# Causal attention on one Trainium2 core: whole-array sums of values and ones, half-wise signals, and a moved output multiply

## The reference

```python
def _L1_attn_ref(x, g1, Wq, Wkv, Wout, g2):
    xn = layernorm(x, g1)
    q = xn @ Wq.T                      # 16 heads of 64
    kv = xn @ Wkv.T
    k, v = (kv[..., :DIM_HEAD], kv[..., DIM_HEAD:])
    ...
    q, k = (l2norm(q), l2norm(k))
    q, k = (q * srt, k * srt)          # srt = 4
    sim = jnp.einsum('bhid,bjd->bhij', q, k)
    causal_mask = jnp.triu(jnp.ones((n, n), dtype=bool), 1)
    sim = jnp.where(causal_mask, max_neg, sim)
    attn = jax.nn.softmax(sim.astype(jnp.float32), axis=-1).astype(sim.dtype)
    out = jnp.einsum('bhij,bjd->bhid', attn, v)
    out = out.transpose(0, 2, 1, 3).reshape(b, n, HEADS * DIM_HEAD)
    return layernorm(out @ Wout.T, g2)
x = _layernorm(x + _L1_attn_ref(x, ...), axis=-1)
```

## Time and profile before

| | us |
|---|---|
| median of 3 runs | 3532.06 |
| lowest and highest of them | 3529.45, 3533.05 |
| the profiled execution | 3527.5 |
| its span, first to last instruction | 3525.8 |
| ACT in the span | 2002.8 busy (57%) |
| DVE | 1776.7 busy (50%) |
| PE | 3118.4 busy (88%) |

### The profile page before, as it was taken

One profiled execution on the slowest core, in us unless ns is written; L12 is line 12 of the kernel. 1 busy time (PEld: TensorE's weight loads), 2 busy tenths in 40 slices (PEclk: granted clock), 3 DMA queues, 4 the chain that ended last, 5 costly groups with the idle time before them and its releaser, 6 DMA issues. The chain is left out here.

```text
span 3525.8 us, 44249 instructions
## 1 busy us (share of the span) xinstructions
PE 3118.4 (88%) x12438; PEld 1661.3 (47%) x12438; DVE 1776.7 (50%) x2639; ACT 2002.8 (57%) x3736; POOL 1152.1 (33%) x954
## 2 busy tenths in 40 slices
PE   5777777789999999966669999999998879999999
PEld 2333332257777777732224444444444634444443
DVE  5888888845555555569953333333333321111110
ACT  4666666446666666635657777777775523333333
POOL 4766776612222222236633333333332000000000
PEclk8999999989999999988889999999999989999999
DMA  3444444300000000001100000000000310000000
GB/s 108 136 137 131 136 138 134 106 16 22 21 16 21 18 20 21 14 27 51 45 36 10 14 17 13 13 13 18 13 13 27 125 42 18 18 21 24 18 18 15
DMA packets 104264, 159.17 MB, mean 45 GB/s; under 512 B 11904, under 2 KB 44560, under 8 KB 104208
## 3 DMA queue, kind: packets, MB, share of 16 engines
q1 hardware_dynamic: 97872, 144.89, 12.5%
q10 hardware_dynamic: 6336, 13.60, 1.4%
HBM read 85.77 MB, written 4.72 MB: 26 GB/s over the span
## 5 line engine op out<-in xcount | busy, mean ns | idle before, releaser
L1364 POOL TENSOR_TENSOR d_pr<-d_pr,d_keep 128x512 f32<-128x512 f32 x256 | 320.5, 1274 | 565.6 <-ACT d_pr L1522 565.6
L779 POOL TENSOR_TENSOR b_pn<-b_e,b_inv 128x616 f32<-128x616 f32 x128 | 161.5, 1261 | 602.9 <-DVE b_inv L960 602.9
L257 POOL TENSOR_TENSOR a_bx<-a_bcopy,a_drive_u 128x512 f32<-128x512 f32 x256 | 320.2, 1268 | 18.8 <-DVE a_state L532 18.0
L532 DVE TENSOR_TENSOR_SCAN a_state<-a_decay,a_bx 128x512 f32<-128x512 f32 x256 | 310.9, 1214 | 1.3 <-POOL a_bx L257 1.3
L277 PE MATMUL a_py<-a_prod,consts 128*128 128x512 f32 x512 | 296.7, 664 | 3.8 <-DVE a_t L512 3.1
L449 ACT ACTIVATE a_decay<-a_delta,neg_a 128x508 f32<-128x508 f32 x256 | 174.4, 683 | 145.3 <-DVE a_state L532 143.6
L1917 PE MATMUL f_ph<-f_hb,wb 128*128 128x512 f32 x512 | 232.8, 599 | 6.4 <-ACT f_hb L1952 6.4
L1917 PE MATMUL f_ph<-f_ha,wb 128*128 128x512 f32 x512 | 229.0, 596 | 2.3 <-DVE f_ha L1981 2.3
L289 PE MATMUL a_pc<-a_bc,sel 96*128 96x512 bf16 x256 | 109.9, 429 | 126.2 <-DVE a_prod L538 124.5
L935 DVE TENSOR_REDUCE b_peak<-b_pscore 128x8 f32<-128x616 f32 x128 | 102.3, 799 | 214.2 <-PE b_pscore L816 214.2
L885 ACT ACTIVATE b_yy<-b_py,y_bias 128x154 f32<-128x154 f32 x512 | 169.4, 382 | 66.2 <-PE b_py L825 66.0
(11 more groups left out here) (282 smaller groups left out, 6563.8 us busy)
## 6 DMA issues: line engine op xcount, KB each, us to landing
a_bcopy<-rows SPq DMA_DIRECT2D x256, 256.0 KB, 3.3
wb<-in_wb ACTq DMA_DIRECT2D x14, 480.0 KB, 3.7
a_xf<-in_x SPq DMA_DIRECT2D x16, 256.0 KB, 3.7
a_xt<-in_x ACTq DMA_DIRECT2D x16, 256.0 KB, 2.9
x<-a_xo SPq DMA_DIRECT2D x16, 256.0 KB, 3.6
b_xf<-x SPq DMA_DIRECT2D x32, 128.0 KB, 2.0
b_xt<-x SPq DMA_DIRECT2D x32, 128.0 KB, 2.0
x<-b_xo SPq DMA_DIRECT2D x32, 128.0 KB, 2.0
```

Of the source, the lines that this page charges most:

```text
L257: gp.tensor_tensor(bx[:, k % 4, :], bcopy[:, k % 4, :], drive_u[:, p, :], ALU.mult).then_inc(*bxt.step("bx"))
L532: V.tensor_tensor_scan(state[:, j % 2, :], decay[j % 2][:], bx[:, j % 4, :], 0.0, ALU.mult, ALU.add).then_inc(*vs.step("scan"))
L779: gp.tensor_tensor(heads(pn[:, j % 2, :]), heads(e[:, j % 2, :]), over(inv[:, j % 2, :], CTX), ALU.mult).then_inc(*pnt.step("n"))
L1364: gp.tensor_tensor(half, half, keep[:].unsqueeze(1).to_broadcast([128, QP, SEQ]), ALU.mult).then_inc(*gmt.step(f"m{odd}"))
```

## The change

It edits `causal_phase` alone.

1. **The sums.** d_vv holds three blocks of 64 columns per sequence, ones, values, ones; POOL fills all of it with ones at the start of the phase, and DVE copies the values into the middle block. `weighted` now has one matmul with 128 stationary columns for the even heads (blocks values, ones) into the first bank of a two-bank d_pattn, and one for the odd heads (blocks ones, values) into the second. Sums and weighted values lie on opposite halves of the partitions in each bank. d_pden and d_ones are gone.
2. **Signals.** Each of the two matmuls has its own signal, a0 and a1. The sums' Ln on ACT is two instructions on 64 partitions each, the first behind a0, the second behind a1; each reads one half of the partitions and writes the other half. The multiply on DVE is two instructions on 64 partitions.
3. **Squares.** Apart from the key's, the squares move to the tick of the projection (QUERY, odd k) and stand between the Ln halves and the Exp of the sums.
4. **Output.** The multiply into d_xo goes from the end of tick 7 to its start on DVE.

```diff
-        vv = sb("vv", [128, 2, NB, DH])
-        ones = sb("ones", [128, DH])
+        vv = sb("vv", [128, 2, NB, 3, DH])
...
-        pattn = ps("pattn")
-        pden = ps("pden")
+        pattn = ps("pattn", 1024)
...
-        pea = tr("pea", "a")
+        pea = tr("pea", "a0 a1")
...
-                gp.memset(ones[:], 1.0).then_inc(*made.step("ones"))
+                gp.memset(vv[:], 1.0).then_inc(*made.step("ones"))
...
-                    for bank, w in ((pattn, vv[:, p, b, :]), (pden, ones[:])):
-                        for odd in range(2):
-                            op = mm(bank[64 * odd:64 * odd + 64, :], w, pr[:, j % 2, odd, :], start=True, stop=True,
-                                    skip_group_check=True)
-                    op.then_inc(*pea.step("a"))
+                    for odd in range(2):
+                        w = vv[:, p, b, 1 - odd:3 - odd, :].rearrange("p i d -> p (i d)")
+                        mm(pattn[:, 512 * odd:512 * (odd + 1)], w, pr[:, j % 2, odd, :], start=True, stop=True
+                           ).then_inc(*pea.step(f"a{odd}"))
...
-                        if u := piece(LENGTH, g, p, k, front, main):
-                            squares(*u)
+                        if k == 3:
+                            if u := piece(LENGTH, g, p, k, front, main):
+                                squares(*u)
...
-                            A(den[:], pden[:], ACT.Ln).then_inc(*sdt.step("ln"))
+                            for odd in range(2):
+                                act.wait_ge(*pea.at(f"a{odd}", r))
+                                op = A(den[64 * odd:64 * odd + 64, :],
+                                       pattn[64 - 64 * odd:128 - 64 * odd, 512 * odd:512 * (odd + 1)], ACT.Ln)
+                            op.then_inc(*sdt.step("ln"))
+                        if k % 2:
+                            if u := piece(QUERY, g, p, k, front, main):
+                                squares(*u)
+                        if done:
                             act.wait_ge(*sdt.at("ln", r))
                             A(den[:], den[:], ACT.Exp, scale=-1.0).then_inc(*sdt.step("inv"))
...
+                        if tail and k == 7:
+                            dve.wait_ge(*so.at("rstd2", g - 1))
+                            if begun(g - 2):
+                                dve.wait_ge(store, 16 * g - 16)
+                            V.tensor_tensor(xo[:, q, :], pm[:, 0:N], t3[:], ALU.mult).then_inc(*vo.step("out"))
...
-                            V.tensor_copy(vv[:, q, :, :], pn[:, 0:NB * DH].rearrange("p (b d) -> p b d", b=NB)
+                            V.tensor_copy(vv[:, q, :, 1, :], pn[:, 0:NB * DH].rearrange("p (b d) -> p b d", b=NB)
...
-                            V.tensor_tensor(attn[:, pu, QP * hh:QP * (hh + 1), SEQ * b:SEQ * (b + 1)],
-                                            pattn[:].rearrange("p (i t) -> p i t", i=QP),
-                                            den[:].rearrange("p (i t) -> p i t", i=QP), ALU.mult
-                                            ).then_inc(*vat.step("n"))
+                            for odd in range(2):
+                                half = slice(64 * odd, 64 * odd + 64)
+                                op = V.tensor_tensor(
+                                    attn[half, pu, QP * hh:QP * (hh + 1), SEQ * b:SEQ * (b + 1)],
+                                    pattn[half, 512 * odd:512 * (odd + 1)].rearrange("p (i t) -> p i t", i=QP),
+                                    den[half, :].rearrange("p (i t) -> p i t", i=QP), ALU.mult)
+                            op.then_inc(*vat.step("n"))
...
-                        if tail and k == 7:
-                            dve.wait_ge(*so.at("rstd2", g - 1))
-                            if begun(g - 2):
-                                dve.wait_ge(store, 16 * g - 16)
-                            V.tensor_tensor(xo[:, q, :], pm[:, 0:N], t3[:], ALU.mult).then_inc(*vo.step("out"))
```

More of the change, by code:

```diff
@@ L1519, in step @@
                             if begun(r - 2):
-                                act.wait_ge(*pea.at("a", r - 2))
+                                act.wait_ge(*pea.at("a1", r - 2))
                             for odd in range(2):
@@ L1523, in step @@
                                   ).then_inc(*ext.step(f"e{odd}"))
-                        if u := summed(g, p, k, main, tail):
-                            _, _, j, r = u
-                            act.wait_ge(*pea.at("a", r))
+                        done = summed(g, p, k, main, tail)
+                        if done:
+                            _, _, j, r = done
                             if begun(r - 1):
                                 act.wait_ge(*vat.at("n", r - 1))
-                            A(den[:], pden[:], ACT.Ln).then_inc(*sdt.step("ln"))
+                            for odd in range(2):
[6 more added lines that the diff above has]
+                                squares(*u)
+                        if done:
                             act.wait_ge(*sdt.at("ln", r))
@@ L1575, in step @@
                             if begun(g - 1):
-                                dve.wait_ge(*pea.at("a", UNITS * g - 1))
-                            V.tensor_copy(vv[:, q, :, :], pn[:, 0:NB * DH].rearrange("p (b d) -> p b d", b=NB)
+                                dve.wait_ge(*pea.at("a1", UNITS * g - 1))
+                            V.tensor_copy(vv[:, q, :, 1, :], pn[:, 0:NB * DH].rearrange("p (b d) -> p b d", b=NB)
                                           ).then_inc(*vf.step("v"))
```

## The result

The changed kernel is slower, by little but clear of the scatter: 3550.85 us (3546.67 to 3553.8) against 3532.56 us of the kernel before, a ratio of 1.0056 with a 95% interval from 1.0041 to 1.0071. The forecast was 3511.5 us, and the range ended at 3533.

The account below looks back on a forecast made before the run. TensorE was taken to bound the causal phase. 0.77 us per group saved, 23.1 us for 30 groups, minus 2.5 us at the ends, gave 20.6 us less: 3532.1 to 3511.5 us, range 3496 to 3533.

Parts of the forecast that it names:

- A: Stretch of a group from `weighted` of unit 3 to that of unit 0: 9.32 us before, 9.06 forecast.
- B: Stretch of a group from `weighted` of unit 0 to that of unit 2: 12.39 us before, 12.09 forecast.
- C: Stretch of a group from `weighted` of unit 2 to that of unit 3: 5.63 us before, 5.47 forecast.
- The loop: From one `weighted` to the next: adds square 0.48 us, second Ln half 0.48 where ScalarE is late, second multiply half 0.69.
- some 0.4 us: Slack in A: the chain ends this long before the output projection wants it, so TensorE's work decides.
- rival 1: ScalarE's halves don't overlap their neighbours: 0.3 us more in B and in C, 3529.5 us; chance 0.22 with its parts.
- both idle times of TensorE: Waits at piece 2's length and at the scores, blamed on ScalarE's late square: 0.8 us per group, expected to go.
- The ends: Last group, where no projection fills TensorE: each unit's loop grows by 0.64 us, four times, 2.5 us more.
- The additions at the changes of tile shape: TensorE around and inside narrow `weighted`: 0.10 us ahead, 0.107 behind, 0.16 inside, 0.36 per unit, all to go.
- rival 2: `weighted` still takes 1.87 us and the additions around it stay: 3532 us; chance 0.09.
- the walk: Following a group through A, B and C: 26.62 us per group; with halves overlapped on VectorE, 3507 us in all.
- Rival 4: Loop shorter than forecast: 3507 us with VectorE halves overlapped, 3468 with TensorE's work alone; chance 0.10 beyond the overlap.

Follow-up runs that it names:

- a_whole_twice2: Changed kernel with both activations (Square for Ln) and both multiplies per unit on all 128 partitions, even heads' results to spare tiles, values differ: 3509.7 us.
- b_squares_out: Kernel before with the squares moved between Ln and Exp of the sums, and the multiply into d_xo first in tick 7: 3512.7 us.
- b_squares: Kernel before with only the squares moved, into their projection's tick between Ln and Exp of the sums: 3519.1 us.
- b_ln_halves: Kernel before with the sums' Ln as two instructions on 64 partitions each, not crossing partitions: 3571.2 us.
- a_whole_once: Changed kernel with one activation (Square for Ln) and one multiply per unit on all partitions, odd heads left out, values differ: 3490.4 us.

## Why the prediction was wrong

**The sum.** For the changed kernel the prediction had 26.62 us per group, and 27.92 were measured, 1.30 more, or 39 us for 30 groups, of the 43.5 us by which the profiled execution missed (3550.4 against 3506.9). By stretches: A 9.29 instead of 9.06, B 12.70 instead of 12.09, C 5.92 instead of 5.47.

**The step that failed** is in "The loop", with its price list: "the second Ln half where ScalarE and not TensorE is late (0.48 again)". In B the first half starts 0.12 us later than 4.31 us behind the scores' Exp, since it doesn't overlap the roots' Exp, and both halves to the square take 1.22 us instead of 0.96, together 0.38 us. In C the square comes 0.33 us later for the same reason. In A it is 0.4 us on the way to the last multiply, which used up the "some 0.4 us" before the output projection and left the wait of 0.15 us there with 0.1 us of weight load behind it. Together that is 0.9 of the 1.30 us per group, some 28 us. It is rival 1 of the prediction, at a larger size: it was given 0.22 and priced at 18 us, with nothing for stretch A and nothing for VectorE's next instruction. a_whole_twice2 shows 41 us for partition changes on both engines together, of which the forecast, with 0.69 us instead of 0.61 for the second multiply half, held 5 already.

**Smaller terms.** The hop from the multiply to `weighted` was taken as 0.04 us from the square's row; measured it is 0.14 to 0.15 (2332.33 to 2332.48, 2338.26 to 2338.40), so the forecast had 0.1 us too little in B and in C. TensorE's own work in B came out 0.1 us larger, since behind an uncovered weight load and at unit 0 `weighted` takes 1.78 us and not 1.71. These 0.3 us per group are 9 us of the error.

**A wrong reading.** The prediction put both idle times of TensorE before, 0.8 us per group, down to the late square. b_squares_out shows that the 0.57 us at the length are the square's and the 0.25 at the scores aren't. It made no difference to this forecast, since in the changed kernel `weighted` waits longer than that ahead of these scores, but it is some 8 of the 10 us that b_squares fell short. And the square's wait was to go in the changed kernel; 0.37 us of it stayed (2330.45), hidden behind the longer wait of the next `weighted`.

**VectorE.** The value of 0.69 us for the second half was right (1.39 for both), and so was the Trainium skill's rule there (VectorE: DVE Perf Modes, Two Vector instructions with no wait between them): an instruction that starts in another quarter of the partitions is held. The runs show the same behaviour on ScalarE: in b_ln_halves a first half that overlaps and a second that doesn't, and d_t's square held, as it seems, by a start partition two instructions back. The prediction named the rule as one against this change and applied it to VectorE only.

**The ends** were given 2.5 us; the phase's last part, from the last key's projection to the next phase's first table load, grew by 5 us (2665.5 to 2720.3 us before, 2682.0 to 2741.8 after). Up to the last group's first `weighted` that is 0.7 us. The last group's loops from unit to unit grow by 1.3 us together: two of the three by 0.63 and 0.69 us, as forecast (the last is 2719.09 to 2723.90, 4.81 instead of 4.12 us), the middle one not at all, since it had 4.84 us before, behind other waits. The other 3 us come behind the last `weighted`, 2.5 of them up to the end of the output projection, where the clock is down: TensorE waits 2.86 us ahead of this `weighted`, and then runs at half its clock:

```profile
2719.09 1.96 PE L1392 MATMUL d_pattn<-d_pr,d_vv 128*128 128x512 f32 x4 [0.54 <-DVE d_attn L1605]
2723.90 3.75 PE L1392 MATMUL d_pattn<-d_pr,d_vv 128*128 128x512 f32 x4 [2.86 <-DVE d_attn L1605]
```

```profile
2719.00:2723.00 4.00, 1.96 (x4) 0.68 (x4) 1.06 (x2) 2.58 (x5) 2.07 (x2) 1.00 0.09 33
2724.00:2727.00 3.00, 3.00 (x4) 1.37 (x5) 0.00 (x0) 0.59 (x1) 0.00 (x0) 0.50 0.00 0
```

The granted clock is 1.00 (2.4 GHz) in 2719 to 2723 us and 0.50 (1.2 GHz) in 2724 to 2727, and this `weighted` takes 3.55 us to the output projection instead of 1.8. In the kernel before, with a wait of 2.17 us there, the granted clock was 1.00 in 2705 to 2714 us.

**What was right.** The additions at the changes of tile shape, with 0.36 us per unit, and that they go with the narrow matmuls: a_whole_once confirms them, against rival 2. That the multiply's wait would come, at units 1, 2 and 3. That the whole is bound by the loop and not by TensorE's work. And the sum itself for instructions that overlap: the walk with 0.61 us for the second multiply gave 3507 us, and a_whole_twice2, which meets that assumption, measures 3509.7. That it is so near is in part luck, since per group it has 26.68 us and the walk 26.46. Rival 4's lower end, 25.2 us per group, is answered by a_whole_once: even without halves it has 26.06, since the scores wait for the chain through the roots. Part 4 was booked at nothing; in the kernel before the trace has no wait for it, and it is 0.2 us per group once the square's wait is gone.

**The account.** From 3532: parts 3 and 4 take off 19 us; whole-array matmuls 22 more (3490); a second whole activation and multiply cost 19 (3510); that they are halves on other partitions costs 41 (3551). The differences between kernels are good to some 5 us each.

**The better version** is b_squares_out: the narrow matmuls of before, the squares in their projection's tick, the output first in tick 7. 3512.7 us is 0.55% below the kernel before and 1.1% below the changed one. Whole-array sums could give 22 us more, if a form were found in which values and sums come without half-wise work; none was found here.

## What to carry to other kernels

An edit that saves time on the busiest engine can lose it in the instructions that the new layout wants elsewhere: count their time per column, not per partition, and count the overlap with both neighbours that they lose when their start partition differs. Where an engine is idle by 0.8 us per period, look for the queue that makes it wait, and move the late instruction there, before you touch the busy engine's own work. Follow each wait back by itself: two waits that lie close together had two causes here. Test the parts of a combined change one by one; here two of four carry a gain of 19 us and a third one of 22, and the halves of the fourth cost more than all of them.

## What the runs showed of the hardware

- ScalarE, like VectorE, starts an instruction only behind the end of the earlier ones when its start partition differs: Ln halves 0.59 us apart instead of 0.48, and no overlap with the next. The d_t square in b_ln_halves, held behind an instruction on all partitions, suggests that the last start in PSUM counts by itself; no run isolates that.
- VectorE's reciprocal takes 3.35 us for 64 partitions of 512 float32 columns, against 0.69 for a multiply.
- TensorE's changes between 64-column, 64-row and full-array matmuls cost 0.1 us each way (in the changed kernel the projection takes 0.96 us ahead of the 64-row scores, 2322.01 to 2322.97, and 0.86 ahead of the full-array output projection, 2312.28 to 2313.14), and four narrow matmuls in pairs take 1.87 us where two full ones take 1.72.
- An operation of VectorE with two tiles in SBUF beside one of GpSimd's. The multiply into d_xn takes 0.48 us before and 1.25 us after (medians of 32), where it falls on the mask:

```profile
2316.82 2.68 POOL L1362 TENSOR_TENSOR d_pr<-d_pr,d_keep 128x512 f32<-128x512 f32 x2 [4.53 <-ACT d_pr L1520]
```

Its row is the first of VectorE's above: 2317.11 us, 0.29 us behind the start of the mask on GpSimd. It cost nothing here: d_xn is ready at 2318.36 us, and the key's projection starts only behind the output projection, at 2318.96. In the kernel before, the sum into d_t at 2697.92 us, also of two tiles in SBUF, falls on a mask and takes 1.00 us instead of 0.42. Why it waits isn't shown; that the two share a way into SBUF is argued, not tested.
